# An order of its own for each engine: a table of moved steps beside the common list

## The reference, cut to what matters

```python
x = x + tanh(g_xattn[l]) * xattn_l(layernorm(x), ctx, ...)
x = x + tanh(g_ffn[l]) * ffn_l(layernorm(x), ...)
```

## Time and profile before

| | |
|---|---|
| median of 3 runs | 1026.75 us (1023.87, 1026.75, 1026.85) |
| the profiled execution | 1024.25 us, of which 1022.4 are its span |
| mean granted clock of PE in it | 0.921 |
| instructions | 16912 |

### The profile page before, as it was taken

How to read it: one execution, slowest core, us unless ns; L and a number is a source line. 1 busy time by engine, 2 the same in 40 slices (tenths; PEclk the granted TensorE clock), 3 DMA queues, 4 the chain that set the end, 5 groups by cost and what they waited for, 6 DMA issues and landing times. The chain is left out here.

```text
span 1022.4 us, 16912 instructions
## 1 busy us (share of the span) xinstructions
PE 860.9 (84%) x5288; PEld 668.6 (65%) x5288; DVE 771.4 (75%) x1907; ACT 558.0 (55%) x1077; POOL 306.2 (30%) x507
## 2 busy tenths in 40 slices
PE   4799578689999997799999999889957789976786
PEld 3677456566666664577878788677845568875564
DVE  5799458679999997298989989677855645555697
ACT  2577235447777775456666565576733444323455
POOL 2533222324343433031222122245410333321134
PEclk9899569859999998799999999999977989998999
DMA  4100010000100000020000000200001000000001
GB/s 129 20 2 2 0 26 1 0 22 10 35 25 24 21 21 1 1 45 1 1 1 1 1 1 1 68 1 2 2 1 39 0 1 1 1 1 1 1 11 32
DMA packets 26005, 14.12 MB, mean 14 GB/s; under 512 B 11047, under 2 KB 25406, under 8 KB 25918
## 3 DMA queue, kind: packets, MB, share of 16 engines
q1 hardware_dynamic: 25918, 13.04, 4.7%
HBM read 11.99 MB, written 1.05 MB: 13 GB/s over the span
## 5 line engine op out<-in xcount | busy, mean ns | idle before, releaser
L891 ACT ACTIVATE L_pt<-bank 128x512 f32<-128x512 f32 x224 | 127.0, 597 | 45.8 <-PE bank L765 30.4
L513 POOL TENSOR_TENSOR L_kc<-L_kc_all,const 128x256 fp32r<-128x256 f32 x96 | 58.8, 617 | 150.3 <-PE bank L765 74.7
L1799 POOL TENSOR_TENSOR L1f_xg_lo<-L1f_xg_raw,L1f_xg_hi 128x512 fp32r<-128x512 f32 x32 | 41.4, 1294 | 172.2 <-ACT L1f_xg_hi L1947 161.1
L878 ACT ACTIVATE L_part<-bank,L_bias_ca,const 128x256 fp32r<-128x256 f32 x128 | 68.7, 562 | 42.1 <-PE bank L685 40.9
L1024 DVE TENSOR_REDUCE L_ms<-bank 128x2 f32<-128x512 f32 x128 | 83.6, 684 | 3.9 <-PE bank L714 3.6
L2063 DVE TENSOR_TENSOR L1f_h_lo<-L1f_h,L1f_h_hi 128x512 fp32r<-128x512 f32 x88 | 77.0, 876 | 8.3 <-ACT L1f_h_hi L1952 7.9
L1941 ACT ACTIVATE L1f_a<-bank 128x512 f32<-128x512 f32 x88 | 52.6, 598 | 47.1 <-PE bank L1844 46.7
L1022 DVE TENSOR_REDUCE L_mc<-bank 128x8 f32<-128x512 f32 (+1 forms) x96 | 65.2, 679 | 13.0 <-PE bank L709 6.9
L1952 ACT CAST L1f_h_hi<-L1f_h 128x512 fp32r<-128x512 f32 x88 | 54.3, 617 | 18.3 <-DVE L1f_h L2058 17.3
L1010 DVE SCALAR_TENSOR_TENSOR L_q<-bank,L_bias_c,L_part 128x256 fp32r<-128x256 f32 x96 | 46.0, 480 | 21.6 <-ACT L_part L878 20.1
L714 PE MATMUL bank<-L_k,L_q 32*128 32x256 f32 x256 | 54.8, 340 | 8.6 <-DVE L_ms L1024 5.7
(11 more groups left out here) (427 smaller groups left out, 2647.7 us busy)
## 6 DMA issues: line engine op xcount, KB each, us to landing
L_raw<-in_L_ffn_w_dram SPq DMA_DIRECT2D x8, 176.0 KB, 2.3
L_raw<-in_L_ffn_v_dram SPq DMA_DIRECT2D x8, 176.0 KB, 2.5
L_raw<-in_L_ffn_w_dram SPq DMA_DIRECT2D x6, 192.0 KB, 3.1
x<-in_x_dram SPq DMA_DIRECT2D x4, 256.0 KB, 4.0
mask<-in_mask_Bx1xSxS_ff_dram SPq DMA_DIRECT2D x2, 512.0 KB, 5.6
out_dram<-x SPq DMA_DIRECT2D x4, 256.0 KB, 2.3
const<-in_const_dram SPq DMA_DIRECT2D x1, 964.0 KB, 5.6
ctx_rows<-in_ctx_dram SPq DMA_DIRECT2D x1, 256.0 KB, 2.9
```

The costliest lines, as they stand in the source:

```text
L513: pool.tensor_tensor(kc[:, g], kc_all[:, g, bass.ds(b, 1)].bitcast(F32).to_broadcast([P, GH, S2]), pr.c("head4").unsqueeze(2).to_broadcast ...
L878: last = act.activation(part[:, i].bitcast(F32R), b_proj[:, i * S:(i + 1) * S], ACT.Identity, bias=bias_ca[:, i, g:g + 1], scale=pr.c("ak" ...
L891: act.activation(pt[:, g // 2, (g % 2) * NS + (HEADS_1[i] if own_keys else i)], b_st[(g * NS + i) % 2][:], ACT.Exp, scale=scale).then_inc( ...
```

## The change

`run` takes a table of places and goes through a list that `placed` makes for each engine: the steps of `program` in which this engine has a part, in the same order, but with the steps that the table names taken out and put behind another step (or, behind `None`, at the front). PE, ACT, DVE and POOL get a table each; SP keeps the common order. The waits, the semaphores and the instructions within a step stay as they are, and so does their number.

| | steps | moved | entries |
|---|---|---|---|
| PE | 1542 | 216 | 150 |
| DVE | 1136 | 151 | 113 |
| ACT | 1143 | 142 | 101 |
| POOL | 363 | 50 | 33 |

The moves lie at the start of `att0`, at the seven seams, in the bodies of `ffn0`, `ffn2` and `ffn3`, and in each batch of `att3`. The middles of `att0` (between its second and its sixth batch), `att1` (between its second and its last batch) and `ffn1` (from about its tile 16 to 85) stay as they are. Of the diff, the new function, the calls, and of the tables the entries around the steps that are spoken of below:

```diff
+def placed(program, does, places):
+    own = [at for at in program if at[1] in does[at[0]]]
+    behind = {step: list(steps) for step, *steps in places}
+    moved = {step for steps in behind.values() for step in steps}
+    assert len(moved) == sum(map(len, behind.values())) and moved <= set(own) and not moved & set(behind)
+    return behind.get(None, []) + [step for at in own if at not in moved for step in (at, *behind.get(at, ()))]
...
+PLACES = {
+    "tensor": (
...
+        (('att0', 'maxima', 7, 1), *of("att0", ('pv', 6, 1, 0))),
...
+        (('att0', 'maxima', 7, 3), *of("att0", ('weights', 7, 1, 0))),
+        (('att0', 'on_turn', 6), *of("att0", ('weights', 7, 3, 0)), *of("ffn0", ('turn', 0))),
...
+        (('ffn0', 'logits', 1), *of("att0", ('pv', 7, 1, 0)), *of("ffn0", ('logits', 2)), *of("att0", ('o_turn', 7))),
...
+        (('ffn0', 'up', 1), *of("att0", ('y', 7))),
...
+        (('att1', 'proj', 0, 0), *of("att1", ('p_vg', 0))),
+        (('ffn0', 'y_turn', 3), *of("att1", ('proj', 0, 1))),
...
+        (('att1', 'weights', 7, 2, 4), *of("att1", ('pv', 7, 0, 4)), *of("ffn1", ('turn', 0))),
...
+        (('att1', 'weights', 7, 3, 2), *of("ffn1", ('logits', 0))),
...
+        (('att2', 'p_vc', 1), *of("att2", ('proj', 0, 1))),
...
+        (('att2', 'on_turn', 6), *of("att2", ('y', 6))),
...
+        (('att2', 'y', 7), *of("ffn2", ('up', 1))),
...
+        (('att3', 'weights', 7, 1), *of("att3", ('sums', 7))),
...
+        (('att3', 'divide', 7, 1), *of("ffn3", ('turn', 2), ('logits', 2)), *of("att3", ('y', 7))),
...
+    "vector": (
+        (('att0', 'p_wx', 1), *of("setup", ('context',), ('stats', 0))),
...
+        (('att0', 'proj', 6, 1), *of("ffn0", ('moments', 0))),
+        (('att0', 'maxima', 6, 3), *of("ffn0", ('moments', 1))),
+        (('att0', 'maxima', 7, 1), *of("ffn0", ('moments', 2))),
+        (('att0', 'maxima', 7, 3), *of("ffn0", ('scale', 1), ('prepare',))),
...
+        (('ffn0', 'turn', 1), *of("att1", ('p_wx_zero',), ('p_bias',))),
...
+        (('att1', 'scores', 7, 3, 4), *of("ffn1", ('prepare',)), *of("att1", ('o_norm', 6))),
...
+        (('ffn2', 'moments', 0), *of("att2", ('y', 6))),
...
+        (('ffn2', 'turn', 0), *of("ffn2", ('moments', 2))),
+        (('ffn2', 'scale', 1), *of("att2", ('o_norm', 7)), *of("ffn2", ('scale', 2))),
+        (('ffn2', 'turn', 1), *of("att2", ('y', 7))),
...
+        (('ffn3', 'scale', 1), *of("att3", ('sums', 7))),
...
+    "gpsimd": (
...
+        (('att0', 'keys', 6, 0), *of("ffn0", ('zero',))),
+        (('att0', 'keys', 7, 0), *of("ffn0", ('rstd', 0))),
+        (('att0', 'keys', 7, 3), *of("att0", ('spread', 7))),
+        (('ffn0', 'split', 9), *of("att1", ('p_zero',), ('keys', 0, 0))),
...
+        (('att1', 'o_norm', 6), *of("ffn1", ('prepare',)), *of("att1", ('o_norm', 7))),
...
+        (('att2', 'mask_in', 0), *of("att2", ('p_rstd', 1), ('p_rstd', 2))),
...
+        (('att3', 'keys', 0, 1), *of("att3", ('p_zero',), ('p_rstd', 1))),
...
-        def run(does):
-            for stage, step, *at in program:
-                if step in does[stage]:
-                    does[stage][step](*at)
+        def run(does, places=()):
+            for stage, step, *at in placed(program, does, places):
...
-                run({stage: stages[stage].gpsimd(pool) for stage in stages})
+                run({stage: stages[stage].gpsimd(pool) for stage in stages}, PLACES["gpsimd"])
...
```

More of the change, by code:

```diff
@@ L2716, in build @@
             program = weave(program, of(stage, *stages[stage].order), *CUES.get(stage, ()))
-        def run(does):
-            for stage, step, *at in program:
-                if step in does[stage]:
-                    does[stage][step](*at)
+        def run(does, places=()):
+            for stage, step, *at in placed(program, does, places):
+                does[stage][step](*at)
         with nc.Block() as block:
@@ L2729, in _ @@
             def _(pool):
-                run({stage: stages[stage].gpsimd(pool) for stage in stages})
+                run({stage: stages[stage].gpsimd(pool) for stage in stages}, PLACES["gpsimd"])
             @block.tensor
             def _(pe):
-                run({stage: stages[stage].tensor(pe) for stage in stages})
+                run({stage: stages[stage].tensor(pe) for stage in stages}, PLACES["tensor"])
             @block.scalar
             def _(act):
-                run({stage: stages[stage].scalar(act) for stage in stages})
+                run({stage: stages[stage].scalar(act) for stage in stages}, PLACES["scalar"])
             @block.vector
             def _(dve):
-                run({stage: stages[stage].vector(dve) for stage in stages})
+                run({stage: stages[stage].vector(dve) for stage in stages}, PLACES["vector"])
 def constants():
```

370 lines of the change are left out of this document (added).

## The result

The changed kernel takes 936.01 us (median of four runs, 930.08 to 945.07) against 1025.4 for the kernel before: a ratio of 0.911, with a 95% interval of 0.904 to 0.918. The ratio and its interval leave out the run of 945.07 us, which counts as slow, being more than 1.5% above the fastest. Timed again later, the ratio was 0.906 (0.902 to 0.910). The forecast was 974 us with a range of 942 to 1010; the direction was right, and the gain was 89 us instead of 51. The profiled execution took 930.08 us, with a span of 928.3.

What follows compares the result with a forecast made beforehand. Neither PE nor DVE is full overall; the seams' idle time, partly queued work, was the target. Terms 2 + 10 + 5 + 9 + 4 + 9 + 4 + 6 + 2 = 51 us off 1024.25 give 973.25, taken as 974; range 942 to 1010.

Steps and rivals of the forecast that it cites:

- the slower rival: POOL waits at keys(0,0) ahead of ffn0's last splits, and later work waits behind it: about 1047 us, chance 0.09.
- For each seam I take the idle time that the rows name and a new order resolves: Rule for sizing every seam's term from waits named in the profile rows; the terms sum to 51 us.
- start and `att0` to its sixth output: Start: stats(0) ahead of two preparing steps on DVE, first projections and scores interleaved; 2 us, from -1 to 6.
- `att0` into `ffn0`, and into `att1`: PE's 4.37 and 4.69 us waits and memsets mended, 10 us (4 to 18); ffn0 into att1, 5 (1 to 12).
- `att1` into `ffn1`: PE's waits of 4.76 and 3.08 us mended, plus 1 for slow-clock matmuls: 9 us, from 3 to 13.5.
- `ffn1` into `att2` (and `att2`'s middle): Follow-up steps of the first projection, for which DVE waits 3.91 us, taken sooner: 4 us, from 1 to 7.
- `att2` into `ffn2`, and into `att3` (and its middle): Two DVE-POOL-DVE round trips overlap, 9 us (3 to 16.9); ffn2 into att3 reordered, 4 us (0 to 9).
- `att3` into `ffn3`, and the end: Sums, outputs and routing move, the 7.85 us wait stays: 6 us (1 to 14); the end 2 us (0 to 5).
- Busy time is therefore the same to first order: Whole kernel: no instruction added, removed or resized and no wait changed, so the sum counts idle time only.
- a rival, with 32 us: More than the named gaps: seams' clock goes to 1, two thirds of 47.9 us counts; about 941 us, chance 0.10.
- the rival with little gain: Gaps are chains, not queues, and mended ones only uncover the next: about 999 us, chance 0.16.
- The rule on the shared port: DVE's 1.73 us cast beside POOL's memset in att0 is mostly waiting; between +1.4 and -0.4 us, not counted.

Runs made afterwards that it cites:

- the third: The kernel before with only the entries from att1's y(5) to ffn1's mul(40), the seam att1 into ffn1: 1004.75 us.
- the fifth with the sixth: The kernel before with only the entries for the seams att2 into ffn2 and ffn2 into att3, and POOL's later ones in att3: 1005.57 us.
- the first two: The kernel before with only the entries for att0 into ffn0, ffn0's body and the seam into att1, together: 1002.16 us.
- filler runs: The kernel before with extra PE transposes ahead of first turns of ffn1, ffn2, ffn3: 1024.35 us beside 1025.38; with more transposes, 1028.12 beside 1026.84.

## Why the prediction was wrong

The reading of the old profile held: neither engine was full at the seams, and the idle time stood there. So did the mechanism, work standing behind other work in its engine's queue, and most signs that the prediction gave for it: the first `up` 10 us earlier, the spread directly behind the last keys, the turns' waits gone except the one before `ffn3`, `att1`'s middle as long as before, and 49.23 us in both from `ffn1`'s second to its third output. One sign failed: the seams' windows are not shorter by their terms but, in three places, by twice as much; and the clock in the seams rose, which it had named as a sign of less time than forecast. POOL was not held up in `ffn0`'s body: its wait before the keys that the slower rival feared is 0.72 us.

```profile
152.65 0.62 POOL L513 TENSOR_TENSOR L_kc<-L_kc_all,const 128x256 fp32r<-128x256 f32 x1 [0.72 <-DVE L_kc_all L969]
```

**The step that failed** is "For each seam I take the idle time that the rows name and a new order resolves". It counted the few longest waits of PE as if the rest of a seam's idle time were chains. By the cut above, the terms measure:

| term | taken | measured | PE's idle time less by |
|---|---|---|---|
| start and `att0` to its sixth output | 2 | -0.2 | 1.6 |
| `att0` into `ffn0`, and into `att1` | 10 + 5 | 33.7 | 21.1 |
| `att1` into `ffn1` | 9 | 18.2 | 12.3 |
| `ffn1` into `att2` (and `att2`'s middle) | 4 | 4.4 + 1.4 | 5.1 + 1.4 |
| `att2` into `ffn2`, and into `att3` (and its middle) | 9 + 4 | 24.3 + 2.9 | 19.4 + 2.9 |
| `att3` into `ffn3`, and the end | 6 + 2 | 9.5 | 10.2 |

The lengths are those of one profile each. The first two rows vary most: in the old order the first takes 97.2 to 102.3 us in six profiles, so no gain or loss shows there, and the second gains 26 to 34 us by the profiles above. Of the 43.1 us by which the 94.1 of the span exceed the 51 taken, 22.8 are idle time (73.8 against 51) and 20.3 busy time. The bounds allowed this much idle time (12 to 101.4); what was wrong is the choice within them.

At the first seam the size rested on a misreading of the change as well. The prediction kept the last output of `att0` "behind the first five up steps"; by PE's table it stands behind `up` 1, and the trace has it behind two. The run with DVE's and POOL's tables alone shows the rest: they mended the two waits named and won 2.0 us over equal work, where all four tables won 17.2. The runs of one seam show that the gains are local: the third, and the fifth with the sixth, give their full share alone. Only the first two lean on each other, for 6.6 us beyond their sum.

A second step failed with it: "Busy time is therefore the same to first order". PE's busy time fell by 20.3 us, above all in the three rows in which the granted clock rose (by 12.6, 5.9 and 4.9 us; it rose by 3.1 in the other rows). The prediction had that as a rival, with 32 us, beside the named waits alone; it was never added to a seam's full idle time, so the range ended at 942. That rival's 941 us are near the time measured, but its parts, 51 and 32, are not: the clock went to 0.90, 0.97 and 0.94 and not to 1, and what it gave too much there it lacked in idle time. By the filler runs the clock came with the filled time and would have given next to nothing without it, in the one seam where it rose.

The chain before `ffn3`'s first turn, which spoke for the rival with little gain, was no chain: three entries took the wait away, though the changed kernel, as forecast, still has it. The rule on the shared port (the Trainium skill, SBUF — State Buffer, section "Who interferes with whom") gave 1.4 us to win at the seam and up to 1.8 to lose in batch 6. The trace agrees: the cast takes 1.30 us less, DVE's copy beside the moved memset ends 0.03 us after it, and the step that holds them is 1.28 us longer than without the memset. The Trainium skill's sentence in PSUM — Partial Sum Buffer, section "Engine vs sequencer instructions", on strictly ordered queues was cited for the slower rival, which did not come. The trace agrees with it in the old order's cost: the spread waited behind a deviation until 118.68 us, and comes at 100.32 where it stands ahead of the deviations.

What stays open: how the 15.2 us of the first seam that need PE and ACT divide between the two, since no run has one of the two tables without the other; and what the clock is worth at the first three seams, since no filler was put into the first two and none raised it at the seam into `ffn1`.

## What to carry to other kernels

When several engines work through one common list, count all idle time of the busier engine at a seam as work that may stand in the wrong queue, and call a wait a chain only when its input is late by its own data; look when that input was ready. Price a reordering by the orders of all engines together, since at the first seam DVE's and POOL's alone gave 2.0 of 17.2 us, and neighbouring seams may need each other. Compare windows that hold the same work: the time up to one output also falls when other work is put behind that output. The lower end of a range should add filled idle time and the lower busy time of PE, since here the two came together.

## What was not expected of the hardware

The same program takes different times from run to run. The changed kernel's four first runs lie within 1.6%, against 0.3% for those of the kernel before; the later runs, six and eleven, lie within 1.1% in both, so it is not shown that the fuller kernel varies more. Between the changed kernel's two profiles, 8.9 us of span apart, the second is 3.4 us later at `att0`'s sixth output, then 5.6 us longer up to `att1`'s first and 2.8 in `att1`'s middle, and 2.9 shorter in the rest. Windows from `ffn0`'s last to `att1`'s first output, of the changed kernel's first profile and of its second:

```profile
167.52:228.95 61.43, 57.51 (x406) 39.93 (x407) 53.14 (x115) 38.84 (x79) 18.94 (x36) 0.83 0.07 19
```

```profile
168.56:237.99 69.43, 65.16 (x406) 45.27 (x407) 54.07 (x116) 38.96 (x79) 18.96 (x36) 0.71 0.06 17
190.00:200.00 10.00, 10.00 (x54) 6.05 (x52) 6.78 (x14) 4.75 (x9) 0.62 (x1) 0.50 0.01 2
200.00:210.00 10.00, 9.75 (x54) 6.71 (x54) 5.20 (x10) 4.77 (x9) 0.62 (x1) 0.50 0.00 1
```

The same 406 matmuls take 57.51 us of PE's time at a granted clock of 0.83 and 65.16 at 0.71, and the stretch 61.43 and 69.43 us. In the second profile the clock is at its lower level, 1.2 GHz (0.50), from 190 to 210 us, while PE is busy for 19.75 of these 20 us, and was busy for 9.01 of the 10 us before. So a busy engine was not enough for the upper level here; why not, no run settles.
